# A GroupNorm, attention and alias-free-filter kernel: leaky relu in ScalarE's pass, rows-up products placed between the down-filter's fp32 products, and engine loops written out

## What is computed

```python
x = x + _L0_conv_ref(_gn(x), Wa, ba, Wb, bb, Wv, bv)   # G = A softmax(B)^T, Z = G softmax(V), per head
# layer 1, on _gn(x):
y = _upfirdn2d_sep(x, up_filter, UP, 1, PADDING, float(UP * UP))
y = y + bias[None, :, None, None]
y = jnp.where(y >= 0, y, y * SLOPE) * GAIN             # SLOPE 0.2, GAIN sqrt(2)
y = jnp.clip(y, -CLAMP, CLAMP)
y = _upfirdn2d_sep(y, down_filter, 1, DOWN, (0, 0, 0, 0), 1.0)
x = x + y
```

## Time and profile before

| | us |
|---|---|
| median of 3 runs | 15492.39 |
| lowest and highest run | 15478.86, 15493.5 |
| span of the profiled execution | 15490.4 |
| PE busy | 14319.3 |
| DVE busy | 12597.6 |
| ACT busy | 11639.9 |
| POOL busy | 10946.1 |

### The profile page before, as it was taken

The page is one execution under the profiler, slowest core; times in us unless marked ns, Lnnn a source line. Parts: engine busy times, 40 slices in busy tenths (PEclk is TensorE's granted clock), DMA queues, the critical chain, the costliest instruction groups (busy, mean ns, idle before and its releaser), DMA issues.

```text
span 15490.4 us, 506727 instructions
## 1 busy us (share of the span) xinstructions
PE 14319.3 (92%) x158688; PEld 12344.3 (80%) x158688; DVE 12597.6 (81%) x28093; ACT 11639.9 (75%) x20736; POOL 10946.1 (71%) x16821
## 2 busy tenths in 40 slices
PE   7999999999999999999999999999999999999999
PEld 6788777887778877788777887777887778877788
DVE  7888878888888888888888887888878888788887
ACT  6777777777777777777777777777777777777777
POOL 5677766777667776677766777667776667766677
PEclk9999999999999999999999999999999999999999
DMA  3233222332223322233322333223332223322232
GB/s 86 69 92 99 72 67 69 90 99 74 69 69 86 99 77 69 69 84 99 81 69 69 81 99 84 68 69 80 97 87 69 69 77 96 89 69 70 74 97 53
DMA packets 1998134, 1233.83 MB, mean 80 GB/s; under 512 B 79748, under 2 KB 1931140, under 8 KB 1996804
## 3 DMA queue, kind: packets, MB, share of 16 engines
q1 hardware_dynamic: 1996804, 1217.21, 30.1%
HBM read 570.85 MB, written 268.44 MB: 54 GB/s over the span
## 4 chain that ended last, share of the span: by engine, by line
PE 51%; DVE 23%; issue 13%; ACT 6%; DMA 3%; DVEq 2%; POOL 0%; SPq 0%; ACTq 0%; POOLq 0%
PE ps L1158 51%; DVE nblk L873 4%; DVE z L1055 3%; DVE t L1049 3%; ACT yb L699 3%; DVE nrun L877 2%; DMA p<-t 2%; ACT z L682 2%; DVE mrun L862 2%; DVE srun L861 1%; DVE yb L1100 1%; DVE sth L985 1%; DVE stc L765 1%; DVE bexp L880 1%; DVE xh L1064 1%
## 5 line engine op out<-in xcount | busy, mean ns | idle before, releaser
L1158 PE MATMUL ps<-dn_t,yb 128*128 128x64 f32 (+1 forms) x32768 | 4328.4, 275 | 33.5 <-DVE z L1055 31.9
L1158 PEld LDWEIGHTS ps<-dn_t,yb 128*128 128x128 f32 x32768 | 3995.8, 192 | 84.2 <-DVE z L1055 54.2
L1100 DVE SCALAR_TENSOR_TENSOR yb<-yb 128x532 f32<-128x532 f32 x4096 | 3287.3, 803 | 758.6 <-ACT yb L699 737.1
L699 ACT ACTIVATE yb<-ps,bias_b 128x532 f32<-128x532 f32 x4096 | 2879.2, 704 | 892.0 <-PE ps L1158 786.1
L497 POOL TENSOR_SCALAR yb<-yb 128x532 f32<-128x532 f32 x4096 | 2701.9, 660 | 1101.6 <-DVE yb L1100 1094.4
L1158 PE MATMUL ps<-up,xn 128*128 128x266 f16 x12288 | 2047.5, 277 | 683.7 <-DVE t L1049 640.3
L667 ACT ACTIVATE t<-ps 128x266 f16<-128x266 f32 x4096 | 1578.4, 390 | 995.5 <-PE ps L1158 976.5
L1049 DVE TENSOR_TENSOR t<-ps,t 128x266 f16<-128x266 f32 x4096 | 1717.4, 423 | 616.4 <-ACT t L667 595.2
L1158 PE MATMUL ps<-up_a,t 128*128 128x138 f16 x15360 | 2030.7, 223 | 48.5 <-DMA t<-p 48.1
L1158 PE MATMUL ps<-up_b,t 128*128 128x138 f16 x15360 | 2026.4, 223 | 0.0
L489 POOL TENSOR_TENSOR xh<-xh,pt 128x512 f32 (+1 forms) x992 | 1632.8, 1647 | 473.2 <-DVE pt L908 473.1
(11 more groups left out here) (168 smaller groups left out, 30698.9 us busy)
## 6 DMA issues: line engine op xcount, KB each, us to landing
xc<-in_x SPq DMA_DIRECT2D x512, 512.0 KB, 3.8
xh<-in_x SPq DMA_DIRECT2D x480, 512.0 KB, 4.7
out<-xh SPq DMA_DIRECT2D x480, 512.0 KB, 3.2
p<-t SPq DMA_DIRECT2D x960, 128.0 KB, 2.4
t<-t SPq DMA_DIRECT2D x960, 128.0 KB, 2.4
t<-p SPq DMA_DIRECT2D x960, 128.0 KB, 2.4
xn<-in_x SPq DMA_DIRECT2D x64, 512.0 KB, 5.1
xh<-in_x SPq DMA_DIRECT2D x64, 256.0 KB, 3.1
```

What stands on the lines that cost most here:

```text
L699: act.activation(yb[:, i % YRING, :, :], y_ps[i % 2], ACT.Identity, scale=UPGAIN * GAIN, bias=bias_b[:, bass.ds(c0 + i, 1)]).then_inc(s_y, 1)
L1100: nc.vector.scalar_tensor_tensor(v, v, SLOPE, v, ALU.mult, ALU.max).then_inc(s_lr, 1)
L1158: return nc.tensor.matmul(o, l, r, start=start, stop=stop, skip_group_check=share)
```

## The change

Three things are done.

1. ACT's pass over the columns-up result (L699) and over the remainder rows (L705) uses the function Prelu with alpha 0.2 in place of Identity, so it does the leaky relu as well. DVE's two leaky relu instructions go, with their semaphores; POOL's clamp waits for ACT's pass directly.
2. `up_rows` becomes a generator that issues one product at a time, and `down_rows` takes it: after its first product comes the wait and the first rows-up product, after the second the second, after the third the third. So rows-up of image i stands behind columns-up of image i, no longer ahead of it. In the first batch of a unit, where no rows-down stands at images 0 and 1, the three come in a row behind columns-up.
3. Every `Fori` becomes a Python `range`, so that each engine's program is straight from beginning to end and holds no register arithmetic, and `wait_alone` becomes a plain wait that is carried by the instruction behind it.

```diff
-            with eng.Fori(1, n // unroll - tail) as k:
+            for k in range(1, n // unroll - tail):
...
-            with eng.Fori(0, UNITS - 1) as u:
+            for u in range(UNITS - 1):
...
             def clip_image(g, i, par):
                 v = yb[:, i % YRING, :, :]
-                wait_alone(pool, s_lr, IMG * g + i + 1)
+                pool.wait_ge(s_y, IMG * g + i + 1 + YCREDIT)
...
             def remainder_high(g, par):
                 v = yr[:, par, :]
-                wait_alone(pool, s_yl, g + 1)
+                pool.wait_ge(s_yr, g + 1)
...
-                        act.activation(yb[:, i % YRING, :, :], y_ps[i % 2], ACT.Identity, scale=UPGAIN * GAIN,
+                        act.activation(yb[:, i % YRING, :, :], y_ps[i % 2], ACT.Prelu, scale=UPGAIN * GAIN, alpha=SLOPE,
...
-                            act.activation(yr[:, par, :], o_ps[0:RR, 0:UP], ACT.Identity, scale=UPGAIN * GAIN,
+                            act.activation(yr[:, par, :], o_ps[0:RR, 0:UP], ACT.Prelu, scale=UPGAIN * GAIN, alpha=SLOPE,
...
-                        if i == 1:
-                            remainder_leaky(g, par)
-                        v = yb[:, i % YRING, :, :]
-                        dve.wait_ge(s_y, IMG * g + i + 1 + YCREDIT)
-                        nc.vector.scalar_tensor_tensor(v, v, SLOPE, v, ALU.mult, ALU.max).then_inc(s_lr, 1)
...
-                    mm3(s1_ps[:, 0:UP], xn_2[:, par, 0, i, :], xn_2[:, par, 1, i, :], up_2[:, 0, :], up_2[:, 1, :],
-                        True).then_inc(s_s1, 1)
+                    o, high, low = s1_ps[:, 0:UP], xn_2[:, par, 0, i, :], xn_2[:, par, 1, i, :]
+                    mm(o, high, up_2[:, 0, :], True, True, share=True)
+                    yield
+                    mm(o, high, up_2[:, 1, :], False, True, share=True)
+                    yield
+                    mm(o, low, up_2[:, 0, :], False, True, share=True).then_inc(s_s1, 1)
...
                     for c in range(2):
                         v = slice(c * P, (c + 1) * P)
-                        down(bank[:, (2 * r + c) * H:(2 * r + c + 1) * H], yb[:, i % YRING, 0, v], yb[:, i % YRING, 1, v],
-                             r == 0 and c == 0)
+                        o = bank[:, (2 * r + c) * H:(2 * r + c + 1) * H]
+                        mm(o[:, 0:DA], yb[:, i % YRING, 0, v], dn_t[:, DB - DA:DB], r == 0 and c == 0, True, share=True)
+                        next(rows, None)
+                        mm(o[:, DB0:H], yb[:, i % YRING, 1, v], dn_t[:], False, True, share=True)
+                        next(rows, None)
...
                         if i >= LAG:
-                            down_rows(g, i - LAG, par)
+                            down_rows(g, i - LAG, par, between)
                         elif before(1):
-                            down_rows(g - 1, IMG + i - LAG, 1 - par)
+                            down_rows(g - 1, IMG + i - LAG, 1 - par, between)
+                        else:
+                            for _ in between:
+                                pass
```

More of the change, by code:

```diff
@@ L374, in swap_rows @@
                     if step:
-                        wait_alone(sp, s_swt[half], SWAP * n + 16 * step)
+                        sp.wait_ge(s_swt[half], SWAP * n + 16 * step)
                     sp.dma_start(to, source).then_inc(s_swt[half], 16)
@@ L411, in store_last @@
                     c, stored = last_half[half]
-                    wait_alone(sp, s_o, 2 * NBAT * (u + 1) - 1 + half + OCREDIT)
+                    sp.wait_ge(s_o, 2 * NBAT * (u + 1) - 1 + half + OCREDIT)
                     sp.dma_start(out_row[u, :, c, :], xh[:, c, :]).then_inc(stored, 16)
                 steps(sp, NBAT, 2, batch, 2)
-                wait_alone(sp, s_st[0], 16 * (NBAT // 2 * (u + 1)))
+                sp.wait_ge(s_st[0], 16 * (NBAT // 2 * (u + 1)))
                 if more:
@@ L420, in unit @@
                 store_last(1)
-                wait_alone(sp, s_st[1], 16 * (NBAT // 2 * (u + 1)))
+                sp.wait_ge(s_st[1], 16 * (NBAT // 2 * (u + 1)))
                 if more:
                     load_last(u + 1, 0)
-                wait_alone(sp, s_sl, 16 * (u + 1))
+                sp.wait_ge(s_sl, 16 * (u + 1))
                 if more:
                     load_last(u + 1, 1)
-            with sp.Fori(0, UNITS - 1) as u:
+            for u in range(UNITS - 1):
                 unit(u, True)
@@ L529, in norm_low_half @@
             def norm_low_half(g, par, h):
[L531 to L532 removed]
+                pool.wait_ge(s_xnh, 2 * g + h + 1)
+                pool.wait_ge(s_xs, 2 * g + h + 1)
                 norm_low(par, 2 * h)
@@ L542, in first_batches @@
                 g = NBAT * u + 1
-                wait_alone(pool, s_r1, GROUPS * u + 1)
-                wait_alone(pool, s_xn, 2 * g)
+                pool.wait_ge(s_r1, GROUPS * u + 1)
+                pool.wait_ge(s_xn, 2 * g)
                 for h in range(2):
@@ L575, in attention @@
                 for i in range(2):
-                    wait_alone(pool, s_xh[i], 16 * (NBAT // 2 - 1) * (u + 1))
-                wait_alone(pool, s_xa, 32 * (u + 1))
-                with pool.Fori(0, NBLK // 2) as k:
+                    pool.wait_ge(s_xh[i], 16 * (NBAT // 2 - 1) * (u + 1))
+                pool.wait_ge(s_xa, 32 * (u + 1))
+                for k in range(NBLK // 2):
                     gather_h(u, 2 * k, 0)
                     gather_h(u, 2 * k + 1, 1)
-                wait_alone(pool, s_xl, 16 * 3 * (u + 1))
+                pool.wait_ge(s_xl, 16 * 3 * (u + 1))
                 for par in range(2):
                     spread(u, par, par)
-                with pool.Fori(1, NBLK // 2) as k:
+                for k in range(1, NBLK // 2):
                     for par in range(2):
@@ L819, in _ @@
                 dve.wait_ge(s_xc[i], 16 * XCH // 2)
-            with dve.Fori(0, NBLK) as k:
+            for k in range(NBLK):
                 c_stats(k)
@@ L825, in link @@
                 ins.then_inc(s_small, 1)
-                wait_alone(dve, s_small, done)
+                dve.wait_ge(s_small, done)
             def norm0_stats(n, done):
@@ L1312, in up_columns, with down_rows @@
                     last.then_inc(s_yp, 1)
-                def down(o, la, lb, first):
-                    mm(o[:, 0:DA], la, dn_t[:, DB - DA:DB], first, True, share=True)
-                    return mm(o[:, DB0:H], lb, dn_t[:], False, True, share=True)
-                def down_rows(g, i, par):
+                def down_rows(g, i, par, between=()):
+                    rows = iter(between)
                     pe.wait_ge(s_yc, IMG * g + i + 1)
@@ L1376, in batch @@
                             pe.wait_ge(s_t1, IMG * (g + 1))
+                        between = ()
                         if after(1):
@@ L1379, in batch @@
                             average = first and i == 0 or par and after(3) and i == 4
-                            up_rows(g + 1, i, 1 - par, (lambda: group_average(q, first)) if average else None)
+                            between = up_rows(g + 1, i, 1 - par, (lambda: group_average(q, first)) if average else None)
                         if not first or i:
```

70 lines of the change are left out of this document (29 added, 41 removed).

## The result

The changed kernel takes 15084.26 us (median of 4 runs, 15072.07 to 15088.99), the kernel before 15487.88 in the same comparison. The ratio is 0.974, interval [0.9726, 0.9754]: 403 us less. The forecast was 14580, 910 less. Direction and range held, but less than half of the gain came.

What follows compares the result with a forecast made beforehand. PE's work was the floor, 16.9 of 18.94 us a filter-stage batch, with waits for late DVE on top. Savings of 28.5 us a unit, x 32 = 912, off 15490.4 gave 14578, forecast 14580; range 14250 to 15100.

Steps and rivals of the forecast that it cites:

- SP: SP's exchange of halves: 2.5 us a step, 7.5 for three, ending at 16.3 with the next head at 17.0, so hidden.
- what would show the forecast wrong: Signs: mixed group of 1.2, pass over 0.9 us, long issue waits on PE, or PE waiting for clamp or exchange.
- Interleaving, PE's work: Rows-up products between rows-down passes in the filter stage cover fp32 weight loads: 0.17 us an image, 642 us in all.
- Rival 1: Weight loads don't overlap, or the fp32 and fp16 mix costs what it hides: 18.05 a batch, 15060; chance 0.16.
- The loop and the head's new wait: Rows-up loop 1.77 against PE's work of 1.55 an image; new head wait 0.77 a batch; batch 17.09, 1.85 less.
- Straight code: Register instructions cost little; only the jump back at a unit's end is credited, 0.5 us a unit.
- The sum of 912: Per unit 28.5 us: 13 full intervals 24.0, first 1.5, last 1.8, batch without rows-up 0.7, jump 0.5; x 32.
- The first interval of a unit: A unit's first interval, with two images not interleaved and a one-time chain, gains 1.5 us.
- Prelu: ACT's pass with Prelu takes 704 ns, as with Identity; lower bound 704, upper twice that.
- Rival 2: Prelu is dearer and ACT no longer fits into 1.77; at double, 20.5 a batch, 16250; chance 0.06.
- POOL and code: POOL's work stays near 14.8 a batch; clamp costed at nothing, up to 0.3 a batch if cover is gone.
- rival 3: Straight code is fetched anew; one 3.2 us wait a batch gives 20.3 a batch, 16.2 ms; chance 0.06.

## Why the prediction was wrong, point by point

- **The step that failed: SP.** "A step of the exchange lands 2.4 us after its issue; with the wait and issue between I count 2.5, 7.5 for three ... It is hidden." The start was right: 8.8 after the head was forecast, and from the head at 2749.03 to the issue at 2757.86 it is 8.83. The duration was wrong: 2.4 is the median of 960 first steps, half of which do not stand behind loads. Behind `xh` the mean was 3.25 already before and is 3.71 after, and in the bad cases 5.4. The forecast left 0.7 us of slack, and a first step of 3.85 already takes 1.35 more. Price: 527 us (runs without exchange) against 25 before, so 502 of the 507 us that are missing; one moved load gives 443 back. The section on what would show the forecast wrong did name this wait, but no rival and no part of the chances did.
- **Why it is later than before.** Two things show. The batch is shorter, and the two loads land later (`xh` 6.0 in place of 4.7, also 5.6 against 4.5 in the runs without exchange), so that the first step is done 6.9 us after the load's issue in place of 5.4 to 6.3. The gap between load and step did not shrink: its mean is 3.71 after and 3.11 before. Why the loads land later stays open. Each late exchange may also delay SP's store and the next exchange, but no run shows that apart. In the unit shown the first full intervals are 17.38, 17.35, 17.55, 18.12 and 18.93; later ones go up and down, and one is 22.69. Behind the long waits the clock fell as well, which the forecast had nowhere. Against the run without exchange there are 479 us of waits for `t<-p`, and 194 less for DVE's split (350.4 there), since the exchange is waited for in their place. So some 240 of the 527 us are in neither sum. PE's busy time is longer by 220 us for the same products, and half-clock stretches are 709 us against 171; at half the clock, where products stood twice as far apart, the 538 more can cost at most 269 (an estimate). So the clock may hold most of the 240, but no run took its part alone.
- **Interleaving, PE's work.** Right: 1.06 for the group, 0.17 an image. Rival 1 (no overlap) is refuted by the rows at 2778.31, though it happened to give 15060, close to the measured time, for another reason.
- **The loop and the head's new wait.** Right in size: 0.79 at the head (0.77), 0.45 ahead of `down_columns` (0.43), 0.49 for the loop at the other images (0.34 in the forecast's list), a batch of 17.37 (17.09). On straight code with Prelu and without the exchange the interleaving gives 246 us, since PE's work falls, but the waits grow from 1.04 to 1.73 a batch.
- **Straight code was mis-sized.** "The register instructions run ahead of the engines and cost little", 0.5 a unit, 16 us. The runs show 422 us without exchange (15463 to 15041), 13 a unit. "Issue" waits are a part (75.6 us in the earlier trace rows, 91.4 in the kernel before without exchange); PE's waits for DVE's split fell from 692.9 to 447.4 between the same two kernels, so the rest came mostly through engines that feed PE. Whether loops, register instructions or lone waits cost this, no run shows.
- **The sum of 912 came out by luck.** Without the exchange the change gives 906, but by place in a unit, forecast and profiled runs differ: the 13 full intervals 24.0 and 18.9 (1.45 each, not 1.85), the first 1.5 and 4.6, the last 1.8 and 0.7, and the stretch between two units' intervals 1.2 and 4.2. Prelu and interleaving, to which the forecast gave 1.85 a batch, are worth 484 us together on straight code, about 1.0 a batch. Errors of both signs cancel.
- **The first interval of a unit.** 1.5 was forecast; it fell from 20.0 to 15.8, 4.2. In the runs without exchange it goes from 20.2 to 18.7 with straight code, 17.3 with Prelu and 15.6 with the interleaving.
- **Prelu.** Right. The pass is as long as with Identity, and DVE's L1100 is gone. Rival 2 is out. Groups of instructions after (busy us, mean ns, idle before):

```profile
L691 ACT ACTIVATE yb<-ps,bias_b 128x532 f32<-128x532 f32 x4096 | 2856.7, 698 | 73.6 <-PE ps L1140 69.0
```

- **POOL and code.** Right that POOL costs nothing: no wait for a clamp is among PE's long ones. But its work did not stay near 14.8 a batch; POOL is busy for 24.6 us of two batches in place of 29.8. Instruction fetches grew from 11.45 to 20.81 MB over the run, and PE's waits on "issue" are down to 1.2 us: rival 3 is out. (Its 16.2 ms is 16.1 by its own terms.)

## What to carry to other kernels

A transfer that is hidden is so only at the present pace. Before forecasting a faster one, take each DMA of the chain by its neighbour in the queue, not by the median of its kind, and ask when the transfers ahead of it will have landed. Issue large loads between the steps of a short, waited-for chain, and not right ahead of its first step: here that was worth 443 us, more than the whole change.

A part that shortens one engine's work can cost time until another engine is relieved: the same interleaving was worth +246 us with Prelu and -462 without. Take the parts of a change apart in both orders before a cause is named.

## What was not expected of the hardware

- A 128 KB DMA behind two loads of 512 KB of the same issuing engine was done 6.9 us after the second load's issue in the changed kernel (5.4 to 6.3 in the kernel before), however late it was issued itself up to a gap of 4 us, and takes 2.5 us alone.
- Hardware loops with their register instructions, and waits that stand as instructions of their own, cost 422 us of 15463 together (2.7%), although PE itself is seen waiting on "issue" for only 91.4 in that kernel.
- In a wait of 4.76 us at the head a stretch of half clock (1.2 GHz) began, and behind the wait rows-up products were 0.55 apart in place of 0.29. Half-clock stretches in the whole run: 325 us before, 709 after, 171 without the exchange.
- A fp32 weight load ran under a fp16 product of the same rows: eight fp32 passes and three rows-up products took 1.06 us, where apart they took 1.23.
- ACT's pass with Prelu took 698 ns, with Identity 704.
